# Starting the stationary tiles of a packed convolution and mixing kernel 16 to 64 bytes further in SBUF

## The reference

```python
# layer 0: grouped convolution, 4 groups of 32 channels, 9 taps, plus a context and a bias
x = x + conv1d(x, weight, padding=4, groups=4) + (cond @ c_weight.T)[:, :, None] + bias[None, :, None]
# layer 1: a mixing matrix per sample, from 8 matrices by attention over cond
h = gelu(gelu(cond @ W0 + b0) @ W1 + b1)
att = softmax(h @ W2 + b2)
x = x + einsum('boi,bih->boh', einsum('bk,koi->boi', att, mix_w), x) + (att @ mix_b)[:, :, None]
```

## Time and profile before

| | |
|---|---|
| median of 3 runs | 726.35 us (726.35 to 726.84) |
| profiled execution, its own time | 728.89 us |
| its span, first to last instruction | 726.9 us |
| PE busy | 716.2 us, 99% of the span |
| PE weight loads busy | 701.7 us, 97% |
| POOL, ACT, DVE busy | 546.9, 601.3, 462.2 us |
| DMA | 177.56 MB, mean 244 GB/s |

### The profile page before, as it was taken

The page is one execution under the profiler, slowest core; times in us unless marked ns, Lnnn a source line. Parts: engine busy times, 40 slices in busy tenths (PEclk is TensorE's granted clock), DMA queues, the critical chain, the costliest instruction groups (busy, mean ns, idle before and its releaser), DMA issues.

```text
span 726.9 us, 29222 instructions
## 1 busy us (share of the span) xinstructions
PE 716.2 (99%) x12417; PEld 701.7 (97%) x12417; DVE 462.2 (64%) x411; ACT 601.3 (83%) x458; POOL 546.9 (75%) x592
## 2 busy tenths in 40 slices
PE   8999999999999999999999999999999999999996
PEld 6799999999999999999999999999999999999996
DVE  4897676576776675575575575575575575575543
ACT  5988888878888888888988888888888988888843
POOL 2799999999999999967767767767767767767750
PEclk9999999999999999999999999999999999999999
DMA  6345858768777877877787778777777767767546
GB/s 208 140 152 200 274 202 281 244 213 298 251 250 261 274 253 248 285 244 246 268 280 260 251 272 294 244 238 275 245 242 275 245 238 275 245 243 271 191 151 243
DMA packets 66551, 177.56 MB, mean 244 GB/s; under 512 B 7437, under 2 KB 50008, under 8 KB 50264
## 3 DMA queue, kind: packets, MB, share of 16 engines
q1 hardware_dynamic: 66002, 176.93, 71.5%
q10 hardware_dynamic: 518, 0.17, 0.1%
HBM read 101.57 MB, written 75.50 MB: 244 GB/s over the span
## 4 chain that ended last, share of the span: by engine, by line
PE 81%; POOL 11%; DMA 5%; SPq 1%; issue 1%; DVE 0%; ACT 0%; DVEq 0%; POOLq 0%; ACTq 0%
PE ps L429 60%; PE ps L460 21%; POOL mix_prod L744 4%; POOL mix_prod L739 4%; DMA mix_dram<-mix_parts 3%; POOL mix_sum_f L747 1%; DMA x_in<-in_x_dram 1%; SPq L290 1%; POOL mix_f L751 1%; DMA mix_rep<-mix_dram 1%; POOL mix_parts L757 1%; POOL mix_parts L754 0%; POOL par L734 0%; POOL par L763 0%; ACT x_hi L512 0%
## 5 line engine op out<-in xcount | busy, mean ns | idle before, releaser
L429 PE MATMUL ps<-x_hi,cw_hi 32*128 32x512 f32 x3072 | 406.0, 387 | 0.8 <-ACT x_hi L512 0.5
L429 PE MATMUL ps<-x_hi,cw_lo 32*128 32x512 f32 x3072 | 405.0, 386 | 0.0
L508 ACT ACTIVATE x_ph<-x_in 128x2560 f32<-128x2560 f32 x63 | 318.7, 5060 | 2.7 <-DMA x_in<-in_x_dram 2.2
L612 DVE TENSOR_TENSOR y_lo<-ps,y_hi 128x512 fp32r<-128x512 f32 x256 | 159.1, 683 | 241.1 <-ACT y_hi L521 241.1
L429 PE MATMUL ps<-x_lo,cw_hi 32*128 32x512 f32 x3072 | 275.6, 385 | 0.0
L429 PEld LDWEIGHTS ps<-x_lo,cw_hi 32*128 32x128 f32 x3072 | 240.0, 183 | 2.3 <-issue 0.8
L429 PEld LDWEIGHTS ps<-x_hi,cw_hi 32*128 32x128 f32 x3072 | 219.5, 184 | 3.8 <-issue 1.6
L429 PEld LDWEIGHTS ps<-x_hi,cw_lo 32*128 32x128 f32 x3072 | 219.1, 184 | 1.6 <-issue 0.2
L460 PE MATMUL ps<-y_hi,mix_rep 32*128 32x512 f32 x2048 | 215.1, 384 | 2.1 <-DMA mix_rep<-mix_dram 2.1
L534 ACT ACTIVATE z_out<-ps,par 128x1024 f32<-128x1024 f32 x124 | 146.5, 1242 | 74.5 <-PE ps L460 74.5
L601 DVE TENSOR_TENSOR x_lo<-x_ph,x_hi 128x2560 fp32r<-128x2560 f32 x63 | 190.0, 3016 | 2.1
(11 more groups left out here) (79 smaller groups left out, 94.9 us busy)
## 6 DMA issues: line engine op xcount, KB each, us to landing
x_in<-in_x_dram SPq DMA_DIRECT2D x64, 1024.0 KB, 7.0
out_dram<-z_out SPq DMA_DIRECT2D x63, 1024.0 KB, 5.0
mix_rep<-mix_dram SPq DMA_DIRECT2D x256, 128.0 KB, 2.7
mix_dram<-mix_parts SPq DMA_DIRECT2D x64, 128.0 KB, 5.7
out_dram<-x_in SPq DMA_DIRECT2D x2, 512.0 KB, 4.0
z_out<-in_L_cond_weight_dram SPq DMA_DIRECT2D x1, 512.0 KB, 4.0
cw_nat<-in_L_cond_weight_dram SPq DMA_DIRECT2D x1, 144.0 KB, 2.2
w_sb<-in_L_cond_W_dram ACTq DMA_DIRECT2D x2, 64.0 KB, 5.0
```

The source lines that it names most:

```text
L429: mm = pe.matmul(y_at(s)[:, g, :], w[rows, m, :], x_at(xx[buf(s)], rows, m), start=i == 0, stop=i == CONV - 1)
L508: nc.scalar.activation(x_ph[buf(s)][:, :, :, :], by_lane(x_in[buf(s)]), ACT.Copy).then_inc(x_split_ph, 1)
L612: nc.vector.tensor_tensor(y_lo[s[1]][:, g, :], y_at(s)[:, g, :], y_hi[s[1]][:, g, :].bitcast(F32), ALU.subtract).then_inc(y_lo_made, 1)
```

## The change

A helper returns a slice of a tile that begins some elements into it. `cw_hi` and the three `mix_rep` are declared 64 elements (256 bytes) longer per partition and used from element 4 (`cw_hi`), 8, 12 and 16 (`mix_rep0` to `mix_rep2`) on. `cw_lo`, the moving operands and all other tiles keep their start modulo 256 bytes. No instruction is added or taken away.

```diff
+        def set_in(tile, by, size):
+            return tile[:, by:by + size]
...
-        mix_rep = [sb(f"mix_rep{k}", [P, G, 2, P], F32R) for k in range(3)]
+        mix_rep = [set_in(sb(f"mix_rep{k}", [P, LANES + G * 2 * P], F32R), 8 + 4 * k, G * 2 * P).rearrange(
+            "c (g h o) -> c g h o", g=G, h=2) for k in range(3)]
...
-        cw_hi = sb("cw_hi", [P, M, P], F32R)
+        cw_hi = set_in(sb("cw_hi", [P, LANES + M * P], F32R), 4, M * P).rearrange("c (m o) -> c m o", m=M)
```

## The result

The changed kernel took 733.24 us (median of 13 runs, 730.33 to 734.88), the kernel before 728.19 us in the 13 runs beside it (726.35 to 731.74). The ratio is 1.0056, with a 95% interval of 1.0035 to 1.0076. It is slower: by 4.1 us by the ratio, whose interval is 2.5 to 5.5 us, and by 5.05 us by the medians. I had forecast no change, 726.4 us, in a range of 724.9 to 730.8.

The account below looks back on a forecast made before the run. The prediction took the kernel to be bound by the 226.7 ns between PE's steps. All terms of the change were taken as 0, leaving the span at 726.9 us and the forecast at the 726.4 us median, range 724.9 to 730.8.

Parts of the forecast that it names:

- What bounds the kernel: Claim that PE's distance between steps, 226.7 ns over 3,072 steps, sets the time; only that or an early wait matters.
- The weight loads: Loads from `cw_hi` and `mix_rep` at new starts, 2,304 steps: taken as 0, at most 16.1 us without cover.
- The moving stream: Matmul operand read beside the weights, their relative places shifted 16 to 48 bytes: taken as 0 per step.
- 13.3 ns: Part of each 226.7 ns step beyond 512 columns at 2.4 GHz (213.3 ns), seen at the higher clock alone.
- my 7 ns: Upper bound on a step's loss, from loads of weights 36 bytes apart (154 ns) against adjacent ones (147 ns).
- The reads of the mixing matrix: 256 transfers of 128 KB landing after 2.7 us, now at other starts: taken as 0, at most 4.4 us.
- the prologue: GpSimd clearing `cw_hi` and placing weights from 5.52 to 7.06 us: 0, covered by 1.5 us of slack.
- The slower rival with a stretched stream: Starts off a multiple of 64 lengthen load or stream in PE's steps: 1.9 to 16.1 us; chance 0.08.
- The faster rival: Weights and stream collide in each PE step; moving them apart frees up to 13.3 ns, 30.7 us; chance 0.10.
- The noise: Claim that a measurement of this kernel can tell about 0.2%, 1.5 us, from no change.

Follow-up runs that it names:

- g1: Against the kernel before, only the moving operand of the mixing (`y_hi`, `y_lo`) begins 32 bytes further; not timed, slot 11.00 us.
- g3: Against the kernel before, a 32-byte tile ahead of `x_hi` puts every weight and moving operand 32 bytes later; not timed, slot 10.88 us.
- f3: Against the kernel before, `mix_rep0` begins 64 and `mix_rep1` 128 bytes further; not timed, slots 10.99 and 11.00 us.
- f2: Against the kernel before, all `mix_rep` and the mixing's moving operand (`y_hi`, `y_lo`) begin 32 bytes further; not timed, slots 10.94 and 10.95 us.
- g2: Against the kernel before, `mix_rep0` begins 256 and `mix_rep1` 32 bytes further; not timed, slots 10.89 and 10.96 us.
- h1: Against the kernel before, `cw_hi` and all three `mix_rep` begin 16 bytes further; ratio 1.0169.
- i1: Against the kernel before, all three `mix_rep` begin 16 bytes further, `cw_hi` unmoved; ratio 1.0012.
- i2: Against the kernel before, `cw_hi` and `cw_lo` begin 16 bytes further, the mixing matrices unmoved; ratio 0.9999.
- f4: Against the kernel before, only `cw_hi` begins 32 bytes further; not timed, slot 11.17 us.
- e3: Against the kernel before, `cw_hi` begins 32 bytes and the three `mix_rep` 16 bytes further; ratio 1.0256.

## Why the prediction was wrong

- *What bounds the kernel.* Right. The distance between steps decides, and the loss is found in it alone: 87 ns per slot, 5.5 us over 64 slots. The measured 4.1 us (2.5 to 5.5) and the 5.05 us of the medians agree with that within the noise, and the two profiles are 5.9 us apart from the first to the last load of a mixing matrix, so none of the loss went into the early waits there.
- *The weight loads.* Right in what it said: the loads kept 183 ns, and `cw_hi` at 16 bytes cost nothing by itself.
- *The moving stream.* This is the step that failed. I put its ends at a gain of 13.3 ns and a loss of 7 ns and took 0. Measured were 0 for the 24 steps with `cw_hi` and 7.2 ns for the 12 mixing steps. The nearness of 7.2 to my 7 is luck: that bound came from loads of 32 columns in the prologue, and g1 went past it with 10 ns. My ground for 0 was that at the lower clock "the same loads run beside the same streams" and nothing is lost. But those rows, as every row of before, had distance 0. They could say nothing of another distance at either clock, as the part itself says two sentences earlier.
- *The reads of the mixing matrix* and *the prologue.* Right: 2.7 us to landing in both profiles, 1.9 us of waits against 2.1.
- *The rivals.* The slower rival with a stretched stream named the right sign and the right part, and its sign of being so, slots over 10.9 us, came true. At its 7 ns end it had nearly the right price of a step, but charged 2,304 steps with it, 16.1 us, where 768 steps paid 5.5 us. It did not have the right rule. It blamed a start off a multiple of 64. g3 has only such starts and is free; f3 has none and pays. What counts is where weights and moving operands begin against each other (g1), within a stage and from one stage to the next (f2), and 256 bytes are as good as 0 (g2). I gave it 0.08 and cut the range at 730.8.
- *The faster rival* is refuted as far as these runs go: eight distances and none below 226.7 ns. What the 13.3 ns are is still open.
- *The noise.* I took 0.2% from three runs 0.5 us apart. The same kernel later spread over 9.9 us (723.62 to 733.49). The range, 5.9 us wide, was narrower than the kernel's own spread, and the changed kernel's median lies beyond it.

What remains argued and not shown is the mechanism: that the reads of weights and moving operands get in each other's way in SBUF, in places that repeat every 256 bytes, and don't when they begin at the same place. Nor is it settled whether neighbouring row groups disturb each other or only wait for each other (f2), or what makes both stages slow at 16 bytes; h1, i1 and i2 show that 16 bytes are dear in both stages together, and free in either one with the other at distance 0.

## What to carry to other kernels

Where PE is full and its row groups run side by side, let the weights and the moving operands of all of them begin at the same place modulo 256 bytes. A tile of odd size ahead of all of them is harmless, as g3 shows; one between them can undo it. Here the timed kernels that paid were 0.6% to 2.6% slower. Some differences of 16 bytes were free, but not all, and spreading the starts never made this kernel faster. And when all rows of a trace share a property, such as one alignment, no agreement among them bounds the price of leaving it.

## What was not expected of the hardware

- A matmul of 32 rows and 512 columns took 226.7 ns of its row group's time with all operands at one place modulo 256 bytes, and with other distances up to 10 ns more per mixing step (g1), or 8.1 ns more per convolution step with `cw_hi` 32 bytes off (f4). Distances of 16, 240 and 256 bytes cost nothing where only one stage had them. The weight load's median stayed at 183 ns.
- The Trainium skill (SBUF — State Buffer, on who interferes with whom) says that "PE and ACT never wait on anyone" and that weight loads have a read port of their own. The 1.0256 of e3, in which only the starts of weights differ, does not agree with that as far as PE's own reads are concerned.
- With 16 bytes of distance in both stages (h1) the same code ran slots of 10.88 us and of 11.12 us within one execution.
